# A transformer layer on one core: scale and shift of the first norm applied as x leaves PSUM, the second batch's x loaded early, and q and k laid out by transfers within SBUF

## What is computed

```python
mod = (_silu(L0_c) @ L0_wmod).reshape(4, 6, 1, -1)      # sa, ca, ga, sb, cb, gb
h = _layernorm(x) * (1 + ca) + sa
x = x + ga * attention(h)      # 16 query heads grouped on 4 key heads of 16 channels,
                               # rotary embedding on q and k, causal softmax
h = _layernorm(x) * (1 + cb) + sb
x = x + gb * ffn(h)            # a 256x256 stage with a router, then
                               # silu(h2 @ w_gate) * (h2 @ w_up) @ w_down, 704 wide
```

## Time and profile before

| what | value |
|---|---|
| median of 3 runs | 474.8 us (474.42 to 476.8) |
| time of the profiled execution | 476.08 us |
| its span, first to last instruction | 474.4 us |
| TensorE busy | 442.2 us (93%) |
| VectorE busy | 351.2 us (74%) |
| ScalarE busy | 301.5 us (64%) |
| GpSimd busy | 228.3 us (48%) |
| mean share of the transfers on queue 1, of 16 DMA engines | 10.4% |

### The profile page before, as it was taken

How to read it: one execution, slowest core, us unless ns; L and a number is a source line. 1 busy time by engine, 2 the same in 40 slices (tenths; PEclk the granted TensorE clock), 3 DMA queues, 4 the chain that set the end, 5 groups by cost and what they waited for, 6 DMA issues and landing times.

```text
span 474.4 us, 9509 instructions
## 1 busy us (share of the span) xinstructions
PE 442.2 (93%) x3336; PEld 375.7 (79%) x3336; DVE 351.2 (74%) x772; ACT 301.5 (64%) x622; POOL 228.3 (48%) x296
## 2 busy tenths in 40 slices
PE   7986889978999999999899999989999999999994
PEld 7674565866687789787659999989788799999994
DVE  4869967898984489889846888988867646678541
ACT  2387478685698867346785775457757797655440
POOL 6396538620455451214847324645542635475334
PEclk9987989999999999999999999999999999999999
DMA  6904200000010000010020000010011001001011
GB/s 188 321 9 139 92 7 1 2 0 3 0 33 0 2 1 1 31 61 1 32 78 23 2 1 2 0 47 2 0 37 46 1 0 46 3 1 46 1 46 44
DMA packets 16448, 16.04 MB, mean 34 GB/s; under 512 B 4105, under 2 KB 14798, under 8 KB 16402
## 3 DMA queue, kind: packets, MB, share of 16 engines
q1 hardware_dynamic: 16402, 15.43, 10.4%
HBM read 11.09 MB, written 4.21 MB: 32 GB/s over the span
## 4 chain that ended last, share of the span: by engine, by line
PE 73%; DVE 12%; ACT 5%; POOL 3%; issue 3%; DMA 3%; SPq 1%; POOLq 0%; DVEq 0%; ACTq 0%
PE banks L727 7%; PE banks L799 7%; PE banks L715 7%; PE banks L801 7%; PE banks L800 7%; PE banks L691 5%; PE banks L580 5%; PE banks L582 5%; PE banks L581 5%; PE banks L670 4%; DVE mxp L1180 3%; PE banks L680 2%; PE banks L782 2%; PE banks L763 1%; PE banks L656 1%
## 5 line engine op out<-in xcount | busy, mean ns | idle before, releaser
L799 PE MATMUL banks<-gTh,guhi 128*128 128x256 f32 x352 | 101.1, 287 | 1.6 <-DVE gTl L1252 0.5
L801 PE MATMUL banks<-gTh,gulo 128*128 128x256 f32 x352 | 98.7, 280 | 0.0
L800 PE MATMUL banks<-gTl,guhi 128*128 128x256 f32 x352 | 98.7, 280 | 0.0
L938 ACT ACTIVATE PT<-banks 128x1024 f32<-128x1024 f32 (+3 forms) x96 | 75.2, 811 | 30.9 <-PE banks L715 25.0
L799 PEld LDWEIGHTS banks<-gTh,guhi 128*128 128x128 f32 x352 | 66.4, 189 | 3.5 <-issue 2.4
L800 PEld LDWEIGHTS banks<-gTl,guhi 128*128 128x128 f32 x352 | 66.4, 189 | 0.4
L801 PEld LDWEIGHTS banks<-gTh,gulo 128*128 128x128 f32 x352 | 66.3, 188 | 0.0
L1180 DVE TENSOR_REDUCE mxp<-banks 128x2 f32<-128x1024 f32 (+3 forms) x56 | 61.8, 1143 | 3.7 <-PE banks L691 2.2
L691 PE MATMUL banks<-QKT 128*128 128x512 f32 (+3 forms) x192 | 52.1, 380 | 8.1 <-ACT QKT L916 5.5
L715 PE MATMUL banks<-QKT 128*128 128x512 f32 (+3 forms) x192 | 51.4, 367 | 1.7 <-DVE fft L1267 0.8
L715 PEld LDWEIGHTS banks<-QKT 128*128 128x128 f32 x192 | 30.4, 189 | 24.0 <-issue 20.8
(11 more groups left out here) (181 smaller groups left out, 1123.0 us busy)
## 6 DMA issues: line engine op xcount, KB each, us to landing
xres<-in_L_attn_x SPq DMA_DIRECT2D x8, 512.0 KB, 4.3
out_x<-xres SPq DMA_DIRECT2D x8, 512.0 KB, 3.0
wm_st<-in_L_wmod SPq DMA_DIRECT2D x1, 1024.0 KB, 9.3
modB<-mod_scratch SPq DMA_DIRECT2D x4, 256.0 KB, 3.3
wg_st<-in_L_ffn_w_gate SPq DMA_DIRECT2D x1, 704.0 KB, 5.2
wu_st<-in_L_ffn_w_up SPq DMA_DIRECT2D x1, 704.0 KB, 6.3
xres<-in_L_ffn_w_down SPq DMA_DIRECT2D x1, 640.0 KB, 6.2
wm_st<-in_L_wmod SPq DMA_DIRECT2D x1, 512.0 KB, 5.4
```

The source lines that it names most:

```text
L799: pe.matmul(out_, guhi[:, k, blk, :], gh, start=(m == 0 and k == 0), stop=False)
L800: pe.matmul(out_, guhi[:, k, blk, :], gl, start=False, stop=False)
L801: i = pe.matmul(out_, gulo[:, k, blk, :], gh, start=False, stop=(m == len(blocks) - 1 and k == KB - 1))
L938: act.activation(PT[:, u % 2, 2 * q:2 * q + 2, 0:CH - q0], both("prob", b, n)[:, :, 0:CH - q0], ACT.Exp, scale=float(D) ** -0.5).then_inc( ...
```

## The change

- `xev` applies the first norm's scale and shift as per-partition scale and bias on the transposed x, in two ScalarE instructions (one for each 128 channels). `wts`, `bias`, `biasq` and their tiles are gone, and `qkv` uses the unscaled weights.
- Both halves of the second batch's x are loaded behind the weights, ahead of the wait for `gmod`.
- In `QKT` a pair of heads has its three parts in 96 rows (`MR`), with the maxima of both heads in four rows below them; `mrd` is two transfers.
- In the first batch q and k are laid out by TensorE as before (`thi`, `tlo`, `tstack`, `tstk`), with `stk` now in a part of `PT`. In batches two to four `stack` transposes the unsplit q and k, four transposes for a half; `shi` (ACT) and `slo` (DVE) write the high and the low part to `qkh` and `qkl`; and `qkd` (SP) lays them into `QKT` by 18 transfers within SBUF: six of 32 rows and twelve of 16 rows, of 2 KB each. The first `max` step of each half waits for all 18.
- `rot` shares its memory with `qk`, so `qkvb` of the next half waits for `stack` of this one. `rt` has its own memory.
- `gmod` has three of its instructions in another form, and a zero fill of `stk` on POOL is gone; `vkeys` fills four rows of `QKT` from `omask` in place of two memsets. Six filling matmuls stand ahead of the first `qkv` in place of behind the second `xT`. Two staging tiles lie in `zbuf`.
- `ORDER` is written anew for all batches.

```diff
-HR = 64
-QK = 3 * D
-QKM = QK + 2
+GR = 2 * D
+MR = 3 * GR
...
-WARM, WARM2, WIDE = 14, 6, CH // (2 * KB * B)
+WARM, WIDE = 14, CH // (2 * KB * B)
+FILL = {('qkv', 0): 6}
+QKD = 16 * 3 * (2 + H)
...
+FIRST = ("tstack", "thi", "tlo", "tstk")
+LATER = ("stack", "shi", "slo", "qkd")
...
+rstd1 norm2 hmod ms1 rs1 norm1 a3 xev ms1 rs1 norm1 norm1 norm1 qkvb qkvb rope stack4 shi slo qkv7 qkvb xev ldW wob
+route ms2 hT0 a2 ytm hhi hlo route qkv4 qkvb a5 a6 route route ynT1 ms2 qkd rs2 h2 h2 h2T3 ynev wo1 rope x1 wo2 h2hi
+ms2 woh stack4 shi slo wol h2lo rstd2 ms2 rs2 max0 mxr norm2 max4 max6 max0 mxr mxr mxr qkd x1 gate3 h2 h2 sil max6
+max4 up0 gate2 sil fft ffhi h2T1 up0 mxr mxr mneg mtT7 h2hi h2lo gate6 fft ffhi mrow mrd max2 mxr rstd2 ffl hmod max0
+mxr max4 mxr max2 max4 max0 mxr mxr mxr prob2 exp max4 mxr ms1 max0 prob4 exp mxr max2 mxr prob0 exp max4 max2 mxr
...
+exp pmask norm1 norm1 qkv2 pv pv xev h2 qkv4 ycopy h2T3 xT0 qkvb h2hi ldW wob up5 up6 qkvb rope stack2 shi fft h2 ffhi
+xev h2 gate4 yT7 h2T5 up0 sil xT1 slo h2lo fft fflo h2hi ffhi qkv6 xev ytm norm2 gate3 fft norm2 qkv1 ynT7 qkvb qkvb
+rope h2lo gate0 up2 up1 sil ffhi fflo sil ynev wo7 stack5 gate0 ldB hmod hT6 hmod ffl fft fft qkd shi slo max2 max4
+up1 ffhi ffhi ms1 hhi fflo mxr mxr sil max4 fft ffhi max0 ffl hlo rs1 mxr mxr ms1 max2 mxr x1 fflo max4 mxr mneg gate6
+sil down0 up2 fft down3 ffhi sum sum fflo rs1 fin rstd2 up4 qkd max2 max6 mtT5 max0 mxr mxr store mrow ldx mrd max2
...
-        Wq_b = sb("Wq_b", [P, KB, QKV])
-        bias_q = sb("bias_q", [P, B, QKV])
-        rot = sb("rot", [P, TPC, 2 * H, D])
-
-        stk = sb("stk", [P, TPC, 2 * H, HR])
-
-        rt = stk[:, :, :, 0:4 * HALF].rearrange("p t h (m i) -> p m t h i", m=4)
+
+        rot = qk[:].rearrange("p t h e i -> p t h (e i)")
+        rt = sb("rt", [P, 4, TPC, 2 * H, HALF])
+
+        qkh = sb("qkh", [P, CH], F32R)
+        qkl = sb("qkl", [P, CH], F32R)
+        stk = PT[:, 1].rearrange("p h n -> p (h n)")[:, 0:TPC * 4 * MR].rearrange("p (t q n) -> p t q n", t=TPC, q=4)
+        pairs_of = rot.rearrange("p t (q e) d -> p t q (e d)", e=2)
...
+            for c in range(NC):
+                load_x(1, c)
...
+                elif kind == "qkd":
+                    wait("shi", n + 1)
+                    wait("slo", n + 1)
+                    wait("prob", 0)
+                    at = slice(n * CH, (n + 1) * CH)
+                    for q in range(2):
+                        for g, part in enumerate((qkh, qkh, qkl)):
+                            sp.dma_start(QKT[g * GR:(g + 1) * GR, q, at].bitcast(F32),
+                                         part[q * GR:(q + 1) * GR, :].bitcast(F32)).then_inc(s_qk[n], 16)
+                    for h in range(H):
+                        rows = (H + h) * D
+                        for g, part in enumerate((qkh, qkl, qkh)):
+                            to = g * GR + (h % 2) * D
+                            sp.dma_start(QKT[to:to + D, 2 + h, at].bitcast(F32), part[rows:rows + D, :].bitcast(F32)
+                                         ).then_inc(s_qk[n], 16)
                 elif kind == "mrd":
                     wait("mrow", n + 1)
-                    for h in range(H):
-                        at = HR * (h % 2) + QK
-                        sp.dma_start(QKT[at:at + 2, h // 2, n * CH:(n + 1) * CH].bitcast(F32), mrT[2 * h:2 * h + 2, :]
+                    for q in range(2):
+                        sp.dma_start(QKT[MR:MR + 4, q, n * CH:(n + 1) * CH].bitcast(F32), mrT[4 * q:4 * q + 4, :]
...
-                    pool.memset(V[:], 0.0)
-                    pool.memset(stk[:], 0.0).then_inc(s_const, 1)
+                    pool.memset(V[:], 0.0).then_inc(s_const, 1)
                     pool.wait_ge(s_const, C_ZERO - 1)
-                    pool.memset(stk[:, :, H:2 * H, QK:QKM], 1.0)
                     pool.memset(V[:, :, :, D:D + 1], 1.0).then_inc(s_const, 1)
...
-                    pool.tensor_scalar(rows[:, 2, :], rows[:, 2, :], 1.0, 0.0, ALU.add, ALU.add)
+                    pool.tensor_scalar(rows[:, 2, :], rows[:, 2, :], 1.0, 1.0, ALU.mult, ALU.add)
...
-                elif kind == "bias":
-                    if b == 0:
-                        pe.wait_ge(s_setV, V_MODC)
-                        pe.wait_ge(s_setM, M_SETW)
-                    free(kind, n)
-                    o = of(kind, b, n)
-                    for k in range(KB):
-                        i = pe.matmul(o[:, 0:QKV], modc[:, 0, k, b:b + 1].to_broadcast([P, P]), Wqkv[:, k, :],
-                                      start=(k == 0), stop=(k == KB - 1))
-                    i.then_inc(S["bias"], 1)
...
-                    if b == 0 and n == 1:
-
-                        for _ in range(WARM2):
-                            pe.matmul(bank(7)[:, 0:P], ident[:], ident[:], start=True, stop=True)
...
-                elif kind == "stack":
-                    wait("sthi", 2 * n // TPC + 1)
-                    wait("stlo", 2 * n // TPC + 1)
-                    free(kind, n)
+                elif kind == "tstack":
+                    fill(kind, n)
+                    wait("thi", n * 2 // TPC + 1)
+                    wait("tlo", n * 2 // TPC + 1)
                     o = both(kind, b, n)
                     for t in range(2):
                         for q in range(4):
-                            i = pe.transpose(o[:, t, q * P:(q + 1) * P], stk[:, (2 * n + t) % TPC, 2 * q:2 * q + 2, :
-                                             ].rearrange("p h d -> p (h d)"), ident[:])
+                            i = pe.transpose(o[0:MR, t, q * P:(q + 1) * P], stk[:, (2 * n + t) % TPC, q, :], ident[:])
+                    i.then_inc(S["tstack"], 1)
+                elif kind == "stack":
+                    wait("rope", n + 1)
+                    free(kind, n)
+                    o = of(kind, b, n)
+                    for t in range(TPC):
+                        i = pe.transpose(o[:, t * P:(t + 1) * P], rot[:, t, :, :].rearrange("p h d -> p (h d)"), ident[:])
                     i.then_inc(S["stack"], 1)
                 elif kind == "max":
                     qt, k0, kn, at = MAX_UNITS[n]
...
+                    fill(kind, n)
+                    if b == 0:
+                        wait("tstk", qt // 2 + 1)
+                    else:
+                        pe.wait_ge(s_qk[qt // TPC], QKD * b)
...
-                    act.activation(xTc[:].rearrange("p t k n -> p (t k n)"), of("xT", b, n), ACT.Copy
-                                   ).then_inc(S["xev"], 1)
-                elif kind == "sthi":
+
+                    if b == 0 and n == 0:
+                        act.wait_ge(s_setV, V_MODC)
+                    o = of("xT", b, n).rearrange("p (t k n) -> p t k n", t=2, k=KB)
+                    for k in range(KB):
+                        i = act.activation(xTc[:, :, k, :], o[:, :, k, :], ACT.Identity, bias=modc[:, 0, k, b:b + 1],
+                                           scale=modc[:, 1, k, b:b + 1])
...
+                elif kind == "tstk":
+                    wait("tstack", n + 1)
+                    if n == 0:
+                        act.wait_ge(s_keys, 2)
+                    o = both("tstack", b, n)[0:MR].rearrange("p t (q n) -> p q t n", q=4)
+                    cols = slice(n * PAIR_T, (n + 1) * PAIR_T)
+                    act.activation(QKT[0:MR, 0:2, cols].rearrange("p q (t n) -> p q t n", t=2), o[:, 0:2], ACT.Copy)
+                    for e in range(2):
+                        i = act.activation(QKT[0:MR, 2 + e:2 + H:2, cols].rearrange("p q (t n) -> p q t n", t=2),
+                                           o[:, 2:4], ACT.Copy, scale=hm[0:MR, e:e + 1])
+                    i.then_inc(S["tstk"], 1)
+                elif kind == "shi":
                     wait("stack", n + 1)
-                    earlier("prob", 2 * NP)
-                    if b == 0 and n == 0:
-                        act.wait_ge(s_keys, 1)
-                    o = both("stack", b, n).rearrange("p t (q n) -> p q t n", q=4)
-                    cols = slice(n * PAIR_T, (n + 1) * PAIR_T)
-                    for rows, to, q in ((slice(0, P), slice(0, 2), 0), (slice(0, HR), slice(2, 2 + H, 2), 2),
-                                        (slice(HR, P), slice(3, 2 + H, 2), 2)):
-                        i = act.activation(QKT[rows, to, cols].rearrange("p q (t n) -> p q t n", t=2),
-                                           o[rows, q:q + 2], ACT.Copy)
-                    i.then_inc(S["stk"], 1)
+                    if n > 0:
+                        act.wait_ge(s_qk[n - 1], QKD * b)
+                    elif b > 1:
+                        act.wait_ge(s_qk[NC - 1], QKD * (b - 1))
+                    act.activation(qkh[:], of("stack", b, n), ACT.Copy).then_inc(S["shi"], 1)
...
-                elif kind == "wts":
-                    for k in range(KB):
-                        i = dve.tensor_scalar(Wq_b[:, k, :], Wqkv[:, k, :], modc[:, 1, k, b:b + 1], None, ALU.mult)
```

(19 more changed lines are left out.)

263 lines of the change are left out of this document (123 added, 140 removed).

## The result

The changed kernel takes 477.66 us (median of 14 runs, 475.26 to 481.5), the kernel before 474.79 us beside it. The ratio is 1.0061, with a 95% interval of 1.0037 to 1.0086: slower by 2.9 us, where -6.3 was forecast. The profiled execution took 476.42 us.

The account below looks back on a forecast made before the run. TensorE was taken as the bound, busy 442.2 of 474.4 us. Terms -11.3 (TensorE), -2 (start), -1 (small waits), +5 (transfers), +1 (clock), +2 (covered halves, qkvb) gave -6.3: 468.5 us, 8-in-10 range 458.5 to 480.

Parts of the forecast that it names:

- TensorE work that goes, -11.3: TensorE, all batches: 72 layout transposes (8.5 us) and the bias steps (2.8 us) go; -11.3 us, bounds -10.5 and -12.8.
- work taken from TensorE is worth its full length wherever TensorE isn't waiting: Premise for the whole kernel: TensorE is busy 442.2 of 474.4 us, so removed TensorE work shortens the time in full.
- The bias products, -2.8: TensorE's bias steps ahead of the projections, removed by the change: 3.9 us busy, taken as 2.8 us saved.
- ScalarE, +0.17 us a link and covered: xev as two instructions at 0.385 us lengthens its link by 0.17 us, covered by queued TensorE steps; without cover 2.8 us.
- The start, -2: First batch: the early x load takes its 5.5 us transfer out of the starting chain; -2 us, between 0 and 4.
- The 18 transfers, +5: Link from stack to first max takes 13.3 us at 0.605 an issue; second batch exposes 7.6, net +5 us (0 to +8).
- The rival by a longer issue: SP's issues of the 18 transfers take 0.8 us each, a link 16.8, giving 481 us; chance of slower 0.20.
- The clock, +1: Second batch's score stage: a TensorE stop of 5 us may bring the lower clock; +1 us.
- after 2.65 us of idle it was 0.50: Basis of the clock's price: in the kernel before, TensorE's clock stood at 0.50 for 3 us after that idle.
- The rival "no change": Score stages: saved TensorE time turns into idle because VectorE's row maxima set the pace; 473 to 476 us, chance 0.13.
- the new order itself is a plan, and any of its steps may stand too early: Remark on the rewritten ORDER of all batches, taken as within the other ranges; no size or chance of its own.

Follow-up runs that it names:

- experiment 9: Kernel before with only the early x, seven of eight layout transposes per pair left out: second batch 475.04 us; in a second kernel, batches three and four, 469.91 us.
- experiment 5: Kernel before with only the second batch's x loaded early, behind the weights: 472.66 us (0.9953), and 472.95 us (0.9972) on another chip.
- the mended splice: Changed kernel with batches one and two in before's order, second laid out by TensorE, and gate4 up0 ahead of the third batch's first stack: 478.55 us.
- experiment 1: Changed kernel with twelve of the 18 transfers (the keys) left out in each half of the second batch: 478.13 us, ratio 1.0032.
- The splices: Changed kernel, second batch's stage in before's order, laid out by TensorE; first batch in before's order 479.35, with seam mended 478.55, first batch in new order 476.28 us.

## Why the prediction was wrong, point by point

**TensorE work that goes, -11.3: the work was nearly right, its worth was not.** This is the step that failed: "work taken from TensorE is worth its full length wherever TensorE isn't waiting". The sum took all of it at full length, in stages where TensorE waits and in stages where it is busy 98%, and it is worth its full length in neither. Shown by experiment 9: 3.3 us taken out of the second batch gave nothing back (+2.1 in the medians), and 6.6 us out of batches three and four gave 3.0; the rest became idle time. For the 48 transposes of these two batches, 5.6 us by that price, that makes -2.6. The bias products, -2.8, were worth 0.3 to 1.8 in the old order, since two of the four sets stood in waits for `xev` and `ytm`. The work itself was taken 2.4 us too long (8.9 us went by the estimate above, less than the lower bound of 10.5).

**ScalarE, +0.17 us a link and covered: wrong twice.** I priced the scaled eviction by the 256-column plain form. It is 0.56, the link is 0.53 longer, and TensorE waits 0.42 of it where it stands in the way in the first two batches. It cost 1.8 us by the medians, where nothing was counted. ScalarE's 282 us for 278 are this, too (16.3 us of `xev` for 12.3).

**The start, -2: right.** Alone it is -2.2 and -2.7 us by the medians (-1.3 and -2.2 by the ratios), and the wait for x and the idle of 2.65 us are gone as told. The low clock was not behind that idle but had begun ahead of it (experiment 5).

**The 18 transfers, +5: the link was right, the wait was mis-sized.** 14.3 us for 13.3; issues of 0.63 for 0.605, which was a misreading (four in 2.54 us are 0.635 each, and 18 of those make 11.4 us, for the 11.3 measured); all transfers of batches three and four covered. The idle beside the link is 5.6 us in all, as counted, but only 2.2 of it waits for a transfer. The rest are TensorE's own waits, for an eviction and for `h2` above all, and these covered the link. Taking 12 of the 18 away gave 1 to 1.5 us at the wait. The rival by a longer issue is excluded by the same rows. Of the Trainium skill's rule that many small transfers are better joined (DMA: Bandwidth & Descriptors, Rules for kernel authors): the trace agrees that the size hardly counts here, 2.0 us from issue to landing at 32 and at 64 KB. Leaving out 12 of the 18 saves more issues than joining those 12 could, and it gave 1 to 1.5 us at the wait and nothing that the median shows.

**The clock, +1: too small, by the medians perhaps the largest miss.** The kernel before has a median clock of 0.9885, the changed one 0.974, and in the profiled pair the lower level costs 2.7 us more. Within the repeated changed kernel the time goes from 474.8 us at 0.982 to 479.4 at 0.968, 3.3 us for 0.01; in the mended splice about 4. By this slope the difference between the two kernels is worth 4.8 to 5.8 us, more than the 2.9 us lost. That is worked out and not shown, because no run held the clock and changed the waits. The other way round is shown: the two profiles of the changed kernel, spans 474.7 and 481.4 us, have the same 3248 matmuls. The second is 1.3 us late from its first product on, which is not the clock; 1.5 more come in a stretch at the lower level from 10.1 to 13.5 us, 2.8 in one from 68.1 to 75.0, and 1.5 between 100 and 140 us, where both have such stretches, in different places (0.4 is made good between 48 and 52 us). Behind 140 us nothing is added. Around the middle one, with equal idles ahead of it:

```profile
65.39 0.36 PE L790 MATMUL banks<-Wo_h,yTs 128*128 128x256 f32 x1 [0.58 <-ACT yTo L1004]
...
67.88 1.06 PE L764 MATMUL banks<-PT,V 128*32 128x512 f32 x8
68.87 1.19 PE L752 MATMUL banks<-QKT 100*128 100x512 f32 x4
70.00 1.07 PE L764 MATMUL banks<-PT,V 128*32 128x512 f32 x8
```

```profile
67.81 0.36 PE L790 MATMUL banks<-Wo_h,yTs 128*128 128x256 f32 x1 [0.57 <-ACT yTo L1004]
...
71.55 1.94 PE L764 MATMUL banks<-PT,V 128*32 128x512 f32 x8
73.42 1.89 PE L752 MATMUL banks<-QKT 100*128 100x512 f32 x4
75.24 1.06 PE L764 MATMUL banks<-PT,V 128*32 128x512 f32 x8
```

Which idles bring the lower level isn't settled. The stretch from 101 us follows the row of idles from 86 to 102, and the one in experiment 9 follows the longer idle. But it came in experiment 1 too, where the idle ahead of `max` was half as long, and in the kernel before it had begun ahead of the idle of 2.65 us. So "after 2.65 us of idle it was 0.50" doesn't hold.

**The rival "no change"** was nearest (473 to 476), and its reason was nearest too: saved work turned into idle, in part. Its named bound, VectorE, is wrong for the new order (46.7 us in 60); it is a set of chains. What I had in half a sentence, "the new order itself is a plan, and any of its steps may stand too early", deserved a price.

**Sum of the parts as measured alone**: -2.4 (x) +1.8 -0.3 (scale) -2.6 (transposes, batches three and four) +2 (second batch, 28 transposes where the change takes out 24) = -1.5 us, against +2.9 of the whole. The remaining 4.4 belong to the new order and its clock together. How they are divided stays open.

**A faster version** came out: the kernel before with only the early x, at 0.9953 and 0.9972 on two chips, faster than both. The splices are no faster for certain. Transfers in batches three and four with before's order and eviction, for which experiment 9 gives another 3 us at most, weren't tried.

## What to carry to other kernels

Take the price of removed work from its own stage: if the engine idles there, ask which chain it waits for, and count the removed work as worth nothing until it's shown; even where it is busy 98%, half may be all that comes back. A run that leaves the work out and puts nothing in its place tells that at once. Give the clock a term of its own: here a stretch of 6.9 us at the lower level cost 2.8 us where TensorE had no slack and nothing where it had. To find where time goes between two executions or two kernels with the same matmuls, compare them one by one and look where the distance grows. Take the duration of an eviction from the row with the same function and operands, not from one with the same columns.

## What was not expected of the hardware

An activation of 128x256 from PSUM took 379 ns as a plain copy and 560 ns with per-partition scale and bias; one of 128x512 as a plain copy 593. The two forms also differ in the function (`Copy`, `Identity`), and no run separates that from the operands. Transfers within SBUF cost SyncE 0.59 us to issue at 32 KB, 0.58 to 0.62 at 64 KB, and 2.0 us from issue to landing for both. And the mean granted clock of one and the same kernel went from 0.971 to 0.991 between executions (the mended splice), at 6 to 7 us of difference, while the kernel before kept to 0.98 to 0.995.
